# Attention of a decoder layer in float32: a query pair's high and low parts by one 128-row instruction each, placed by transfers

## The chip, the cores and the metric

One NeuronCore of a Trainium2 chip runs the whole kernel. The metric is the device time of one execution in microseconds (us).

## The reference, cut to what matters

A decoder layer on x of shape (4, 512, 512): self-attention, a cross-attention on 64 tokens, and a top-2 mixture of 8 experts, each behind a layer norm. Only the self-attention is touched:

```python
HQ, HKV, HD = (32, 8, 64)
q = (x @ Wq.T).reshape(B, L, HQ, HD)
k = (x @ Wk.T).reshape(B, L, HKV, HD)
v = (x @ Wv.T).reshape(B, L, HKV, HD)
q = _rope(q)
k = _rope(k)
...
attn = jnp.einsum('bkgqd,bkld->bkgql', qh, kh) * SCALE
attn = jnp.where(causal[None, None, None], attn, -jnp.inf)
p = jax.nn.softmax(attn, axis=-1)
out = jnp.einsum('bkgql,bkld->bkgqd', p, vh)
...
return out @ Wo.T
```

## The kernel before, in words

**Numbers in two parts.** TensorE multiplies in a shorter float format (fp32r), so each operand is split: a high part, which is a copy rounded to that format, and a low part, the value less its high part, rounded again. A product is the sum of the products of parts.

**Order of the work.** The attention stage runs over 8 groups (one key and value head and its 4 query heads), in each over 4 batches, in each over 4 query heads, 128 heads in all. Here `g` is the group, `b` the batch in it, `h` the head in it, `m = 4 g + b` the batch counted through, `n` the head counted through. Every engine has its own program, `pe_group`, `act_group`, `dve_group` and `pool_group`, which states the order of its steps head by head; they meet in semaphores only. The steps are staggered: while TensorE makes the scores of head n + 1, the probabilities of head n are transposed and the output of head n - 1 is made.

**A head's chain.** Scores on TensorE (`pe_scores`, line 207), in four row blocks of 512, 384, 256 and 256 columns into three banks. VectorE adds the causal mask and takes the row's extreme (`dve_masked`, line 421), four instructions. ScalarE takes the exponential (`act_exp`, line 312). VectorE inverts the sums (`dve_recip`, line 428), once per head. GpSimd scales (`pool_norm`, line 545). TensorE transposes ten blocks (`pe_ptrans`, line 217) in three units 0, 1 and 2, of which 0 and 2 share a bank. ScalarE takes the high part of each unit (`act_pt`), VectorE the low part (`dve_pt`, line 409, tile `pt_lo`). TensorE multiplies with v (`pe_pv`, line 234). The output product (`pe_wo`, line 246) follows per batch. In VectorE's order unit 2 of the head before stands behind the masked reductions of the next, and TensorE's unit 0 waits for it.

**The projections.** The next batch's products with the weights (`pe_proj`, line 184) are issued behind the scores of heads 0, 1 and 2: key and value rows (r = 0), the first pair of query heads (r = 1), the second pair (r = 2). As the weights' rows are laid out here `pe_proj` with index 2 is issued at head 0. Head 3 has no projection, but a short transpose of v (`pe_vt`). Rotation of a pair: VectorE multiplies by the cosine and swaps neighbouring rows (`dve_rope_in`, lines 439 and 440), GpSimd multiplies by the sine and adds (`pool_rope`, lines 536 and 538). The result `rope` holds two heads: 64 rows each.

**The query tile.** `q_st` holds for each of the four heads 128 rows: high part and low part, 64 rows each, so that one matmul with the key part takes both. In the first head of a pair the high part lies in rows 0 to 63, in the second in rows 64 to 127; the low part in the other half. `act_rope` (line 315) with r = 1 or 2 writes the high parts with two ScalarE copies of 64 rows (lines 324 and 325). `dve_q_lo` (line 442) writes the low parts with two VectorE subtractions of 64 rows (lines 446 and 447), of which each moves its result to the other half. It stands in VectorE's order behind the masked reductions, `dve_pt` of unit 2 and the low part of an output (`dve_o`, tile `o_lo`), and in front of `dve_rope_in`. The pair r = 1 of the next batch is made in head 2 and needed by the scores issued in head 3; the pair r = 2 of the present batch is made in head 0 and needed by the scores issued in head 1. `pe_scores` waits for `q_lo_done`.

**Weights.** SP loads a group's raw weights (`sp_w1`, `sp_w2`, lines 581 and 587) as soon as the raw tile is free, in a loop over groups; the high and low parts are made in group slots, the low parts of the query, key and value weights by GpSimd (`w1_lo`, line 456, in slots of batch 2), those of the output weights by VectorE in head 2 of batch 1 (`dve_w2`).

**The loop.** Group 0 and group 7 are written out. Groups 1 to 6 are a hardware loop of two passes over three groups each (lines 634, 667, 709, 738): the three probability buffers turn with the head, and 16 heads are one more than a multiple of three.

Of the kernel before, what the change touches and what calls it, by code (L numbers as in the profile page):

```python
# [15 lines left out]
F32 = mybir.dt.float32  # L16
F32R = mybir.dt.float32r
# [4 lines left out]
ALU = mybir.AluOpType  # L22
# [3 lines left out]
P = 128  # L26
# [72 lines left out]
def decoder_layer(nc, x, ctx, ctx_cols, mem_mask, wqkv, wo_rows, router_cols, router_b, gu_w, gu_b, down_w, down_b,  # L99
                  cos_t, sin_t, causal_t, ident_t, iota_t, out):  # L100
    stack = ExitStack()
    with stack:
# [24 lines left out]
        def sa(name, shape, dt=F32):  # L127
# [10 lines left out]
        probs = sa("probs", [P, 3, P_LEN])  # L138
        pt = [[sa(f"pt{b}_hi", [P, PT_LEN], F32R), sa(f"pt{b}_lo", [P, PT_LEN], F32R)] for b in range(2)]
        q_st = sa("q_st", [P, G, L], F32R)  # L140
        k_hi = sa("k_hi", [P, 2, L], F32R)
        k_lo = sa("k_lo", [P, 2, L], F32R)
        v_st = sa("v_st", [P, 2, QB, P], F32R)
# [14 lines left out]
            "const_in", "ident_in", "x_first", "x_in0", "x_in1", "x_in2", "x_in3", "zero_done", "half_done",  # L158
            "stat_done", "aggr_done", "eps_done", "rstd_done", "norm_done", "lnt_done", "ln_hi", "ln_lo",
            "w1_in", "w2_in", "w1_hi_done", "w1_lo_done", "w2_hi_done",  # L160
            "w2_lo_done", "proj_done", "vt_done", "rope_in", "rot_sin", "rope_sum", "rope_hi", "k_lo_done", "q_lo_done",
            "v_tr", "v_hi_done", "v_lo_done", "scores_done", "masked_done", "exp_done",
            "recip_done", "pnorm_done", "ptrans_done", "pt_hi_done", "pt_lo_done", "pv_done", "opart_done",
            "oadd_done", "o_hi_done", "o_lo_done", "wo_done", "wo_out_done")}
# [32 lines left out]
        def pe_scores(pe, n, m, h, kb):  # L197

            pe.wait_ge(s["k_lo_done"], 2 * m + 2)
            pe.wait_ge(s["q_lo_done"], 2 * m + 1 + (h >= 2))  # L200
            for k, blocks in enumerate(((3,), (2,), (1, 0))):
                wait(pe, s["masked_done"], 4 * n - (3, 2, 0)[k])
                for i in blocks:
                    cols = P * (i + 1) if i else 2 * P
                    at = 2 * P if i == 0 else 0
                    for a, kk in enumerate((k_hi, k_lo)):
                        last = nc.tensor.matmul(S_BANK[k][:, at:at + cols], q_st[:, h, i * P:(i + 1) * P], kk[:, kb, 0:cols],  # L207
                                                start=(a == 0), stop=(a == 1))
                last.then_inc(s["scores_done"], 1)
# [105 lines left out]
        def act_rope(act, m, r, mb):  # L315

            act.wait_ge(s["rope_sum"], 3 * m + r + 1)
            if r == 0:
                wait(act, s["scores_done"], 12 * m - 12)
                act_split(k_hi[0:HD, mb, :], rope[0:HD, mb, :], s["rope_hi"])  # L320
                act_split(k_hi[HD:P, mb, :], rope[0:HD, mb, :], s["rope_hi"])
            else:
                wait(act, s["scores_done"], 12 * m - 12 + 6 * r)
                act_split(q_st[0:HD, 2 * r - 2, :], rope[0:HD, (mb + r) % 2, :], s["rope_hi"])
                act_split(q_st[HD:P, 2 * r - 1, :], rope[HD:P, (mb + r) % 2, :], s["rope_hi"])

        def act_vt(act, m, r_sem_value):
            act.wait_ge(s["proj_done"], r_sem_value)
# [112 lines left out]

        def dve_q_lo(dve, m, r, mb):

            dve.wait_ge(s["rope_hi"], 6 * m + 2 * r + 2)
            a, c = 2 * r - 2, 2 * r - 1
            nc.vector.tensor_tensor(q_st[HD:P, a, :], rope[0:HD, (mb + r) % 2, :], q_st[0:HD, a, :].bitcast(F32), ALU.subtract)
            nc.vector.tensor_tensor(q_st[0:HD, c, :], rope[HD:P, (mb + r) % 2, :], q_st[HD:P, c, :].bitcast(F32), ALU.subtract).then_inc(s["q_lo_done"], 1)

        def dve_v(dve, m, vb):
            dve.wait_ge(s["v_hi_done"], m + 1)  # L450
# [95 lines left out]

        def pool_k_lo(pool, m, mb):

            pool.wait_ge(s["rope_hi"], 6 * m + 2)
            wait(pool, s["pnorm_done"], 16 * m - 8)  # L550
            for half_ in range(2):
                nc.gpsimd.tensor_tensor(k_lo[half_ * HD:(half_ + 1) * HD, mb, :], rope[0:HD, mb, :], k_hi[0:HD, mb, :].bitcast(F32),
                                        ALU.subtract).then_inc(s["k_lo_done"], 1)
            pool.wait_ge(s["k_lo_done"], 2 * m + 2)
# [26 lines left out]
        def sp_w1(sp, g):  # L581
# [2 lines left out]
                settled(sp)  # L584
            sp.dma_start(w1_raw[:, :, :], wqkv[bass.ds(g * P, P), :, :]).then_inc(s["w1_in"], 16)

        def sp_w2(sp, g):
            wait(sp, s["w2_lo_done"], 2 * g)
            if not isinstance(g, int):
                settled(sp)  # L590
            sp.dma_start(w2_raw[:, :, :], wo_rows[bass.ds(g * P, P), :, :]).then_inc(s["w2_in"], 16)

        with nc.Block() as block:

            @block.sync
            def _(sp):
                sp.dma_start(x_res[:, 0:1, :], xr[:, 0:1, :]).then_inc(s["x_first"], 16)
                sp.dma_start(x_res[:, 1:QB, :], xr[:, 1:QB, :]).then_inc(s["x_in0"], 16)
                sp_w1(sp, 0)
                for b in range(1, B):  # L600
                    sp.dma_start(x_res[:, b * QB:(b + 1) * QB, :], xr[:, b * QB:(b + 1) * QB, :]).then_inc(s[f"x_in{b}"], 16)
                    if b == 1:
                        sp.dma_start(cos[:, :], cos_t).then_inc(s["const_in"], 16)
                        sp.dma_start(sin[:, :], sin_t).then_inc(s["const_in"], 16)
                sp.dma_start(causal[:, :], causal_t).then_inc(s["const_in"], 16)
                sp_w2(sp, 0)
                with sp.Fori(1, GROUPS) as g:
                    sp_w1(sp, g)
                    sp_w2(sp, g)

            @block.tensor
            def _(pe):
                pe.wait_ge(s["ident_in"], 16)
                pe.wait_ge(s["zero_done"], 4)
                for t in range(TT):
                    pe_ln(pe, t)
                    if t == 6:
                        pe.wait_ge(s["w1_lo_done"], 3)
                        pe.wait_ge(s["ln_lo"], QB)
                        pe_proj(pe, 0, 2)  # L620
                    if t == 9:
                        pe.wait_ge(s["rope_in"], 1)
                        pe.wait_ge(s["vt_done"], 1)
                        pe_proj(pe, 0, 0)
                    if t == 12:
                        pe.wait_ge(s["rope_in"], 2)
                        pe_proj(pe, 0, 1)
                    if t == 14:
                        pe.wait_ge(s["rope_in"], 3)
                        pe_vt(pe, 0)  # L630
                pe.wait_ge(s["ln_lo"], TT)
                pe_scores(pe, 0, 0, 0, 0)
                pe_group(pe, 0, 0)
                with pe.Fori(0, (GROUPS - 2) // 3) as q:
                    for i in range(1, 4):
                        pe_group(pe, 3 * q + i, i % 3)
                pe_group(pe, GROUPS - 1, (GROUPS - 1) % 3)
                pe_ptrans(pe, HEADS * GROUPS - 1, (HEADS * GROUPS - 1) % 3, 2)
                pe_pv(pe, HEADS * GROUPS - 1, B * GROUPS - 1, 1, 1)
                pe_wo(pe, B * GROUPS - 2, 0, 3)  # L640
                for t in range(QB):
                    pe_wo(pe, B * GROUPS - 1, 1, t, (*S_BANK, PJ_BANK)[t])

            @block.scalar
            def _(act):
# [18 lines left out]
                act_rope(act, 0, 2, 0)  # L664
                act_exp(act, 0, 0)
                act_group(act, 0, 0)
                with act.Fori(0, (GROUPS - 2) // 3) as q:
                    for i in range(1, 4):
                        act_group(act, 3 * q + i, i % 3)
                act_group(act, GROUPS - 1, (GROUPS - 1) % 3)  # L670
                act_pt(act, HEADS * GROUPS - 1, 1, 2)
                act_opart(act, HEADS * GROUPS - 1)
# [3 lines left out]
            def _(dve):  # L676
# [29 lines left out]
                dve_masked(dve, 0, 0)  # L706
                dve_recip(dve, 0, 0)
                dve_group(dve, 0, 0)
                with dve.Fori(0, (GROUPS - 2) // 3) as q:
                    for i in range(1, 4):  # L710
                        dve_group(dve, 3 * q + i, i % 3)
                dve_group(dve, GROUPS - 1, (GROUPS - 1) % 3)
                dve_pt(dve, HEADS * GROUPS - 1, 1, 2)
                dve_oadd(dve, HEADS * GROUPS - 1, 1, HEADS * GROUPS // 2 - 1)
# [5 lines left out]
            @block.gpsimd  # L720
            def _(pool):
                nc.gpsimd.memset(half[:, :], -0.5).then_inc(s["half_done"], 1)
                pool.wait_ge(s["half_done"], 1)
                for t in range(TT):
                    wait(pool, s["lnt_done"], t - 1)
                    ln_norm(nc, pool, s, "", t, x_res[:, t, :], ln_out[:, t % 2, 0:D], var_eps, half, rstd)
                    if t == 10:
                        pool.wait_ge(s["const_in"], 48)
                        pool_rope(pool, 0, 0, 0)
                    if t == 12:  # L730
                        pool.wait_ge(s["norm_done"], 13)
                        pool_k_lo(pool, 0, 0)
                    if t == 14:
                        pool_rope(pool, 0, 1, 0)
                pool_rope(pool, 0, 2, 0)
                pool_norm(pool, 0, 0)
                pool_group(pool, 0, 0)
                with pool.Fori(0, (GROUPS - 2) // 3) as q:
                    for i in range(1, 4):
                        pool_group(pool, 3 * q + i, i % 3)  # L740
                pool_group(pool, GROUPS - 1, (GROUPS - 1) % 3)

        attn.close()
# [894 lines left out]
```

## Time and profile before

| | |
|---|---|
| median of 3 runs | 1640.2 us (1631.22, 1640.2, 1640.63) |
| the profiled execution | 1635.06 us |
| its span, first to last instruction | 1633.3 us |
| TensorE matmul (PE) busy | 1483.1 us, 91% |
| TensorE weight load (PEld) busy | 1306.6 us, 80% |
| VectorE (DVE) busy | 1372.1 us, 84% |
| ScalarE (ACT) busy | 1057.7 us, 65% |
| GpSimd (POOL) busy | 849.6 us, 52% |

The attention stage takes the first two thirds of the span. Matmuls overlap and their ends are modelled, so a busy TensorE is not one at its peak. "SPq" is SP's queue, which issues the transfers. In groups by line the last columns are the busy time, the mean of one instruction, and the time that the engine stood idle just before these instructions with what ended most of it. In the timeline "[1.51 <-DVE pt_lo L409]" is idle time before the instruction and what ended it. The granted clock (PEclk) is TensorE's, as a share of its full speed of 2.4 GHz.

### The profile page before, as it was taken

Reading aid. Unit: us, or ns where it says so; the run is one execution under the profiler, and the core shown is the slowest. Engines: PE = TensorE matmul, PEld = TensorE weight load, DVE = VectorE, ACT = ScalarE, POOL = GpSimd, SP = SyncE. Lnnn points to the kernel's source line nnn. Section 1 sums busy time; section 2 is a strip of 40 time slices with the busy share of each in tenths; the row PEclk is TensorE's granted clock in tenths of the full one; section 3 lists DMA queues with packets and bytes.
Section 4 is the critical chain, followed back from the end, with each engine's and each line's share of the span. In section 5 each row is a group of like instructions: output and inputs, shape, how many; then the busy total and the mean of one; then the engine's idle time right before and its main releaser. Section 6 shows DMA issues by size and latency. Waiting matters only on the chain. (4 is left out here: it accounts for less than half of the span.)

```text
span 1633.3 us, 31312 instructions
## 1 busy us (share of the span) xinstructions
PE 1483.1 (91%) x8951; PEld 1306.6 (80%) x8951; DVE 1372.1 (84%) x3565; ACT 1057.7 (65%) x2464; POOL 849.6 (52%) x1033
## 2 busy tenths in 40 slices
PE   5789999999999899999999999688599999999994
PEld 4678888888888788878878877577489999999993
DVE  7789888898898788988988988577579988998892
ACT  3677777777777677777777777332166666666661
POOL 6667657657657557657657655267612233222321
PEclk9899999999999999999999999967599999999997
DMA  4000000000000000000000000112468778887765
GB/s 175 1 14 20 1 14 21 1 14 21 1 14 20 3 14 21 2 14 21 1 14 1 1 1 1 41 65 92 164 184 243 226 217 220 240 228 219 198 172 135
DMA packets 62032, 124.97 MB, mean 77 GB/s; under 512 B 20942, under 2 KB 21070, under 8 KB 61792
## 3 DMA queue, kind: packets, MB, share of 16 engines
q1 hardware_dynamic: 51408, 102.24, 19.6%
q0 software_dynamic: 10304, 20.59, 6.6%
q8 instruction: 77, 1.26, 0.3%
q14 instruction: 99, 0.81, 0.2%
q10 hardware_dynamic: 144, 0.07, 0.0%
HBM read 106.08 MB, written 24.71 MB: 80 GB/s over the span
## 5 line engine op out<-in xcount | busy, mean ns | idle before, releaser
L312 ACT ACTIVATE probs<-probs,neg_max 128x512 f32<-128x512 f32 (+3 forms) x512 | 281.7, 552 | 46.5 <-DVE neg_max L421 44.2
L545 POOL TENSOR_SCALAR probs<-probs,row_inv 128x512 f32<-128x512 f32 (+3 forms) x512 | 264.3, 535 | 44.4 <-DVE row_inv L428 44.4
L536 POOL TENSOR_TENSOR rot<-rot,sin 128x512 f32<-128x512 f32 (+1 forms) x96 | 123.6, 1288 | 303.4 <-DVE rot L440 299.1
L217 PE MATMUL bank<-ident,probs 128*128 128x128 f32 x1280 | 184.5, 275 | 59.6 <-DVE pt_lo L409 50.1
L409 DVE TENSOR_TENSOR pt_lo<-bank,pt_hi 128x512 fp32r<-128x512 f32 (+1 forms) x384 | 216.3, 591 | 25.8 <-ACT pt_hi L305 25.7
L305 ACT ACTIVATE pt_hi<-bank 128x512 fp32r<-128x512 f32 (+1 forms) x384 | 186.3, 518 | 71.6 <-PE bank L217 63.6
L421 DVE CUSTOM_DVE_ANT_0 probs<-bank,causal 128x512 f32<-128x512 f32 (+3 forms) x512 | 219.7, 482 | 10.1 <-issue 3.6
L1221 POOL DMA_INDIRECT acc<-ctx_raw,idx x46 | 74.5, 1619 | 294.9 <-ACT ctx_raw L1374 280.8
L217 PEld LDWEIGHTS bank<-ident,probs 128*128 128x128 f32 x1280 | 149.9, 140 | 94.9 <-DVE pt_lo L409 54.9
L1302 PE MATMUL bank<-xt_hi,gu_hi 128*128 128x256 f32 x736 | 208.4, 283 | 2.0 <-DVE xt_lo L409 1.5
L1302 PE MATMUL bank<-xt_lo,gu_hi 128*128 128x256 f32 x736 | 206.7, 281 | 0.0
L1302 PE MATMUL bank<-xt_hi,gu_lo 128*128 128x256 f32 x736 | 206.5, 281 | 0.0
L207 PE MATMUL bank<-k_hi,q_st 128*128 128x256 f32 (+2 forms) x512 | 172.3, 347 | 3.2 <-DVE xn_lo L409 3.2
L234 PE MATMUL bank<-pt_hi,v_st 128*128 128x256 f32 (+2 forms) x512 | 171.4, 346 | 1.6 <-DVE pt_lo L409 1.6
L207 PE MATMUL bank<-k_lo,q_st 128*128 128x256 f32 (+2 forms) x512 | 156.9, 328 | 0.0
L234 PE MATMUL bank<-pt_lo,v_st 128*128 128x256 f32 (+2 forms) x512 | 155.8, 326 | 0.0
L184 PE MATMUL bank<-xn_hi,w_hi 128*128 128x512 f32 x384 | 153.2, 399 | 0.4 <-DVE rot L440 0.4
L184 PE MATMUL bank<-xn_lo,w_hi 128*128 128x512 f32 x384 | 151.9, 396 | 0.0
L184 PE MATMUL bank<-xn_hi,w_lo 128*128 128x512 f32 x384 | 151.5, 395 | 0.0
L1302 PEld LDWEIGHTS bank<-xt_hi,gu_hi 128*128 128x128 f32 x736 | 139.2, 189 | 6.2 <-issue 2.8
L1302 PEld LDWEIGHTS bank<-xt_lo,gu_hi 128*128 128x128 f32 x736 | 139.5, 189 | 2.8
L1302 PEld LDWEIGHTS bank<-xt_hi,gu_lo 128*128 128x128 f32 x736 | 139.1, 189 | 0.0
(196 smaller groups left out, 3912.8 us busy)
## 6 DMA issues: line engine op xcount, KB each, us to landing
gu_raw<-in_gate_up SPq DMA_DIRECT2D x92, 512.0 KB, 4.2
dn_raw<-in_down SPq DMA_DIRECT2D x92, 256.0 KB, 3.8
w_raw<-in_wqkv SPq DMA_DIRECT2D x8, 768.0 KB, 4.1
w_raw<-in_wo_rows SPq DMA_DIRECT2D x8, 512.0 KB, 3.5
h_rows<-ln_h SPq DMA_DIRECT2D x16, 256.0 KB, 2.0
acc<-x_res SPq DMA_DIRECT2D x4, 1024.0 KB, 4.7
x_res<-in_x SPq DMA_DIRECT2D x3, 1024.0 KB, 11.4
ctx_raw<-in_ctx SPq DMA_DIRECT2D x2, 512.0 KB, 6.7
```

Source lines behind the costliest of these rows:

```text
L184: last = nc.tensor.matmul(PJ_BANK[:, :], w1[sp][:, c, r * P:(r + 1) * P], xn[mp][:, c, b * L:(b + 1) * L], start=first, stop=(c == DC - 1 ...
L207: last = nc.tensor.matmul(S_BANK[k][:, at:at + cols], q_st[:, h, i * P:(i + 1) * P], kk[:, kb, 0:cols], start=(a == 0), stop=(a == 1))
L217: last = nc.tensor.transpose(T_BANK[u % 2][:, k * P:(k + 1) * P], probs[:, hb, P_AT[i] + j * P:P_AT[i] + (j + 1) * P], ident[:, :])
L234: last = nc.tensor.matmul(dst, v_st[:, vb, j, :], rhs, start=(j == 0 and a == 0), stop=(j == QB - 1 and a == 1))
L305: nc.scalar.activation(dst, src, ACT.Copy).then_inc(sem_, 1)
L312: nc.scalar.activation(row, row, ACT.Exp, bias=neg_max[:, hb, i:i + 1], scale=-1.0, accum_out=row_sum[:, hb, i:i + 1]).then_inc(s["exp_don ...
L409: nc.vector.tensor_tensor(dst, src, hi.bitcast(F32), ALU.subtract).then_inc(sem_, 1)
L421: nc.vector.tensor_tensor_reduce(out=probs[:, hb, P_AT[i]:P_AT[i] + (i + 1) * P], in0=S_BANK[k][:, at:at + (i + 1) * P], in1=causal[:, (QB ...
L536: nc.gpsimd.tensor_tensor(rot[0:rows, :], rot[0:rows, :], sin[0:rows, :], ALU.mult).then_inc(s["rot_sin"], 1)
L545: nc.gpsimd.tensor_scalar(row, row, row_inv[:, hb, i:i + 1], 0.0, ALU.mult, ALU.add).then_inc(s["pnorm_done"], 1)
L1221: nc.gpsimd.indirect_dma_start(out=acc, out_offset=bass.IndirectOffsetOnAxis(ap=idx[:, 2 * tau + h:2 * tau + h + 1], axis=0), in_=y[:, 2 * ...
L1302: last = nc.tensor.matmul(GU_BANK[u % 3][:, side * TILE:(side + 1) * TILE], gu[sp_][:, ib, c, side, :], xts[mp][:, k, c, :], start=first, ...
```

## The change

Each part of a query pair is now made by one instruction over all 128 rows, into two new tiles, `q_two` high and low, in the order in which `rope` holds the pair. ScalarE copies the high part, VectorE subtracts the low part, and then SP issues four transfers of 64 rows from `q_two` to the places in `q_st` (`sp_q`). The scores wait for these transfers, `q_in1` or `q_in2`, in place of `q_lo_done`. The wait for the scores that last read `q_st` moves from ScalarE to SP; ScalarE waits for the transfers that last read `q_two`. The loops over groups are written out on all engines, and SP's program is an order by batches, in which the weights' loads stand between the query transfers. Since q's high parts have a semaphore of their own, `pool_k_lo` waits for another count. The same four lines stand in the programs of ScalarE, VectorE and GpSimd as shown for TensorE.

```diff
--- before.py
+++ after.py
@@ -138,6 +138,7 @@
         probs = sa("probs", [P, 3, P_LEN])
         pt = [[sa(f"pt{b}_hi", [P, PT_LEN], F32R), sa(f"pt{b}_lo", [P, PT_LEN], F32R)] for b in range(2)]
         q_st = sa("q_st", [P, G, L], F32R)
+        q_two = [sa("q_two_hi", [P, L], F32R), sa("q_two_lo", [P, L], F32R)]
         k_hi = sa("k_hi", [P, 2, L], F32R)
         k_lo = sa("k_lo", [P, 2, L], F32R)
         v_st = sa("v_st", [P, 2, QB, P], F32R)
@@ -158,7 +159,7 @@
             "const_in", "ident_in", "x_first", "x_in0", "x_in1", "x_in2", "x_in3", "zero_done", "half_done",
             "stat_done", "aggr_done", "eps_done", "rstd_done", "norm_done", "lnt_done", "ln_hi", "ln_lo",
             "w1_in", "w2_in", "w1_hi_done", "w1_lo_done", "w2_hi_done",
-            "w2_lo_done", "proj_done", "vt_done", "rope_in", "rot_sin", "rope_sum", "rope_hi", "k_lo_done", "q_lo_done",
+            "w2_lo_done", "proj_done", "vt_done", "rope_in", "rot_sin", "rope_sum", "rope_hi", "k_lo_done", "q_hi_done", "q_lo_done", "q_in1", "q_in2",
             "v_tr", "v_hi_done", "v_lo_done", "scores_done", "masked_done", "exp_done",
             "recip_done", "pnorm_done", "ptrans_done", "pt_hi_done", "pt_lo_done", "pv_done", "opart_done",
             "oadd_done", "o_hi_done", "o_lo_done", "wo_done", "wo_out_done")}
@@ -197,7 +198,7 @@
         def pe_scores(pe, n, m, h, kb):
 
             pe.wait_ge(s["k_lo_done"], 2 * m + 2)
-            pe.wait_ge(s["q_lo_done"], 2 * m + 1 + (h >= 2))
+            pe.wait_ge(s["q_in2" if h >= 2 else "q_in1"], 64 * m + 64)
             for k, blocks in enumerate(((3,), (2,), (1, 0))):
                 wait(pe, s["masked_done"], 4 * n - (3, 2, 0)[k])
                 for i in blocks:
@@ -320,9 +321,11 @@
                 act_split(k_hi[0:HD, mb, :], rope[0:HD, mb, :], s["rope_hi"])
                 act_split(k_hi[HD:P, mb, :], rope[0:HD, mb, :], s["rope_hi"])
             else:
-                wait(act, s["scores_done"], 12 * m - 12 + 6 * r)
-                act_split(q_st[0:HD, 2 * r - 2, :], rope[0:HD, (mb + r) % 2, :], s["rope_hi"])
-                act_split(q_st[HD:P, 2 * r - 1, :], rope[HD:P, (mb + r) % 2, :], s["rope_hi"])
+                if r == 2:
+                    act.wait_ge(s["q_in1"], 64 * m + 64)
+                else:
+                    wait(act, s["q_in2"], 64 * m)
+                act_split(q_two[0][:, :], rope[:, (mb + r) % 2, :], s["q_hi_done"])
 
         def act_vt(act, m, r_sem_value):
             act.wait_ge(s["proj_done"], r_sem_value)
@@ -441,10 +444,8 @@
 
         def dve_q_lo(dve, m, r, mb):
 
-            dve.wait_ge(s["rope_hi"], 6 * m + 2 * r + 2)
-            a, c = 2 * r - 2, 2 * r - 1
-            nc.vector.tensor_tensor(q_st[HD:P, a, :], rope[0:HD, (mb + r) % 2, :], q_st[0:HD, a, :].bitcast(F32), ALU.subtract)
-            nc.vector.tensor_tensor(q_st[0:HD, c, :], rope[HD:P, (mb + r) % 2, :], q_st[HD:P, c, :].bitcast(F32), ALU.subtract).then_inc(s["q_lo_done"], 1)
+            dve.wait_ge(s["q_hi_done"], 2 * m + r)
+            dve_lo(q_two[1][:, :], rope[:, (mb + r) % 2, :], q_two[0][:, :], s["q_lo_done"])
 
         def dve_v(dve, m, vb):
             dve.wait_ge(s["v_hi_done"], m + 1)
@@ -546,7 +547,7 @@
 
         def pool_k_lo(pool, m, mb):
 
-            pool.wait_ge(s["rope_hi"], 6 * m + 2)
+            pool.wait_ge(s["rope_hi"], 2 * m + 2)
             wait(pool, s["pnorm_done"], 16 * m - 8)
             for half_ in range(2):
                 nc.gpsimd.tensor_tensor(k_lo[half_ * HD:(half_ + 1) * HD, mb, :], rope[0:HD, mb, :], k_hi[0:HD, mb, :].bitcast(F32),
@@ -584,6 +585,15 @@
                 settled(sp)
             sp.dma_start(w1_raw[:, :, :], wqkv[bass.ds(g * P, P), :, :]).then_inc(s["w1_in"], 16)
 
+        def sp_q(sp, m, r):
+
+            sp.wait_ge(s["q_lo_done"], 2 * m + r)
+            wait(sp, s["scores_done"], 12 * m - 12 + 6 * r)
+            a, c = 2 * r - 2, 2 * r - 1
+            for dst, of in ((q_st[0:HD, a, :], q_two[0][0:HD, :]), (q_st[HD:P, a, :], q_two[1][0:HD, :]),
+                            (q_st[0:HD, c, :], q_two[0][HD:P, :]), (q_st[HD:P, c, :], q_two[1][HD:P, :])):
+                sp.dma_start(dst.bitcast(F32), of.bitcast(F32)).then_inc(s[f"q_in{r}"], 16)
+
         def sp_w2(sp, g):
             wait(sp, s["w2_lo_done"], 2 * g)
             if not isinstance(g, int):
@@ -604,9 +614,15 @@
                         sp.dma_start(sin[:, :], sin_t).then_inc(s["const_in"], 16)
                 sp.dma_start(causal[:, :], causal_t).then_inc(s["const_in"], 16)
                 sp_w2(sp, 0)
-                with sp.Fori(1, GROUPS) as g:
-                    sp_w1(sp, g)
-                    sp_w2(sp, g)
+                sp_q(sp, 0, 1)
+                sp_q(sp, 0, 2)
+                for m in range(1, B * GROUPS):
+                    if m % B == 1 and m // B + 1 < GROUPS:
+                        sp_w1(sp, m // B + 1)
+                    if m % B == 3 and m // B + 1 < GROUPS:
+                        sp_w2(sp, m // B + 1)
+                    sp_q(sp, m, 1)
+                    sp_q(sp, m, 2)
 
             @block.tensor
             def _(pe):
@@ -631,9 +647,8 @@
                 pe.wait_ge(s["ln_lo"], TT)
                 pe_scores(pe, 0, 0, 0, 0)
                 pe_group(pe, 0, 0)
-                with pe.Fori(0, (GROUPS - 2) // 3) as q:
-                    for i in range(1, 4):
-                        pe_group(pe, 3 * q + i, i % 3)
+                for g in range(1, GROUPS - 1):
+                    pe_group(pe, g, g % 3)
                 pe_group(pe, GROUPS - 1, (GROUPS - 1) % 3)
                 pe_ptrans(pe, HEADS * GROUPS - 1, (HEADS * GROUPS - 1) % 3, 2)
                 pe_pv(pe, HEADS * GROUPS - 1, B * GROUPS - 1, 1, 1)
...
```

## Rows read from the trace of the kernel before

**Rows 1.** Busy time by stretch: us, PE, PEld, DVE, ACT, POOL (instructions), PEclk, DMA, GB/s.
```profile
275.00:375.00 100.00, 95.94 (x551) 83.18 (x551) 88.85 (x241) 76.56 (x193) 63.23 (x82) 1.00 0.02 7
```

**Rows 2.** Groups by line, 75 to 1100 us: count, busy us, mean ns, idle before.
```profile
L217 PE MATMUL bank<-ident,probs 128*128 128x128 f32 x1260 | 181.5, 275 | 55.7 <-DVE pt_lo L409 46.2 <-POOL probs L545 8.8 <-issue 0.5
...
L305 ACT ACTIVATE q_st<-rope 64x512 fp32r<-64x512 f32 x122 | 76.4, 626 | 2.2
...
L409 DVE TENSOR_TENSOR o_lo<-o_f,o_hi 128x512 fp32r<-128x512 f32 x64 | 46.9, 733 | 0.7 <-ACT o_hi L305 0.7
```

**Rows 3.** Timeline, batch 2's heads 0 and 1: start us, us, engine, line, operation.
```profile
356.35 0.48 PE L207 MATMUL bank<-k_hi,q_st 128*128 128x512 f32 x1
...
357.20 0.69 DVE L421 CUSTOM_DVE_ANT_0 probs<-bank,causal 128x512 f32<-128x512 f32 x1
...
359.90 0.68 DVE L446 TENSOR_TENSOR q_st<-rope,q_st 64x512 fp32r<-64x512 f32 x1
...
364.12 0.48 PE L207 MATMUL bank<-k_hi,q_st 128*128 128x512 f32 x1
```

**Rows 4.** Timeline, a group's batch 0, heads 2 and 3.
```profile
313.97 0.69 DVE L446 TENSOR_TENSOR q_st<-rope,q_st 64x512 fp32r<-64x512 f32 x1
...
318.11 0.48 PE L207 MATMUL bank<-k_hi,q_st 128*128 128x512 f32 x1
...
319.08 0.67 DVE L421 CUSTOM_DVE_ANT_0 probs<-bank,causal 128x512 f32<-128x512 f32 x1
```

**Rows 5.** Timeline, the same group's batch 1, heads 2 and 3, with SP's queue.
```profile
344.19 0.69 DVE L446 TENSOR_TENSOR q_st<-rope,q_st 64x512 fp32r<-64x512 f32 x1
...
345.61 1.29 DVE L409 TENSOR_TENSOR w_lo<-w_raw,w_hi 128x512 fp32r<-128x512 f32 x2
...
347.13 0.33 SPq L591 DMA_DIRECT2D w_raw<-in_wo_rows  x1
...
349.15 0.49 PE L207 MATMUL bank<-k_hi,q_st 128*128 128x512 f32 x1
...
350.50 0.67 DVE L421 CUSTOM_DVE_ANT_0 probs<-bank,causal 128x512 f32<-128x512 f32 x1
```

**Rows 6.** Timeline, the same group's batch 2, heads 2 and 3.
```profile
375.00 1.72 POOL L456 TENSOR_TENSOR w_lo<-w_raw,w_hi 128x512 fp32r<-128x512 f32 x1
...
375.61 1.66 DVE L446 TENSOR_TENSOR q_st<-rope,q_st 64x512 fp32r<-64x512 f32 x1
...
380.33 0.49 PE L207 MATMUL bank<-k_hi,q_st 128*128 128x512 f32 x1
```

**Rows 7.** DMA issues, and stretches: a 128-partition store, the 64-partition ctx loads.
```profile
h_rows<-ln_h SPq DMA_DIRECT2D x16, 256.0 KB, 2.0
...
1076.71:1076.96 0.25, 0.25 (x5) 0.25 (x4) 0.25 (x3) 0.25 (x2) 0.21 (x1) 1.00 1.00 385
...
1057.20:1057.60 0.40, 0.00 (x0) 0.00 (x0) 0.00 (x0) 0.00 (x0) 0.40 (x2) 0.50 1.11 215
```

**Rows 8.** Timeline, the first and last pair: q's low part, then scores or reduction.
```profile
44.90 0.68 DVE L446 TENSOR_TENSOR q_st<-rope,q_st 64x512 fp32r<-64x512 f32 x1
...
48.03 0.80 PE L207 MATMUL bank<-k_hi,q_st 128*128 128x512 f32 x1 [3.22 <-DVE xn_lo L409]
...
1010.87 0.68 DVE L446 TENSOR_TENSOR q_st<-rope,q_st 64x512 fp32r<-64x512 f32 x1
...
1014.81 0.67 DVE L421 CUSTOM_DVE_ANT_0 probs<-bank,causal 128x512 f32<-128x512 f32 x1
```

**Rows 9.** Reciprocals of groups 3, 4 and 5, and a stretch after the restart.
```profile
414.92 0.18 DVE L428 RECIPROCAL row_inv<-row_sum 128x4 f32<-128x4 f32 x1 [0.99 <-ACT probs L312]
...
537.94 0.18 DVE L428 RECIPROCAL row_inv<-row_sum 128x4 f32<-128x4 f32 x1 [0.99 <-ACT probs L312]
...
666.52 0.18 DVE L428 RECIPROCAL row_inv<-row_sum 128x4 f32<-128x4 f32 x1 [0.99 <-ACT probs L312]
...
553.00:556.00 3.00, 3.00 (x12) 2.67 (x11) 3.00 (x11) 2.53 (x6) 2.92 (x6) 0.56 0.00 0
```

More of the change, by code:

```diff
@@ L666, in _ @@
                 act_group(act, 0, 0)
-                with act.Fori(0, (GROUPS - 2) // 3) as q:
-                    for i in range(1, 4):
-                        act_group(act, 3 * q + i, i % 3)
+                for g in range(1, GROUPS - 1):
+                    act_group(act, g, g % 3)
                 act_group(act, GROUPS - 1, (GROUPS - 1) % 3)
@@ L708, in _ @@
                 dve_group(dve, 0, 0)
-                with dve.Fori(0, (GROUPS - 2) // 3) as q:
-                    for i in range(1, 4):
-                        dve_group(dve, 3 * q + i, i % 3)
+                for g in range(1, GROUPS - 1):
+                    dve_group(dve, g, g % 3)
                 dve_group(dve, GROUPS - 1, (GROUPS - 1) % 3)
@@ L737, in _ @@
                 pool_group(pool, 0, 0)
-                with pool.Fori(0, (GROUPS - 2) // 3) as q:
-                    for i in range(1, 4):
-                        pool_group(pool, 3 * q + i, i % 3)
+                for g in range(1, GROUPS - 1):
+                    pool_group(pool, g, g % 3)
                 pool_group(pool, GROUPS - 1, (GROUPS - 1) % 3)
```

## The prediction

> **What bounds the kernel now.** I read the busy time by stretches first: in 100 us from the middle of the attention stage TensorE is busy for 95.94 us, VectorE for 88.85, ScalarE for 76.56, at a granted clock of 1.00 [rows 1]. So TensorE bounds this stage and VectorE stands close behind it. Then the groups of instructions by line: the only work that TensorE waits for is the transpose of the probabilities, 55.7 us of idle time in front of it, 46.2 of them until VectorE's pt_lo [rows 2]. The timeline says where. A batch is four heads of one group of weights. Heads 0 to 2 issue a projection of the next batch behind their scores; head 3 has none, and there TensorE stands until VectorE has done the head's four masked reductions and pt_lo. That is a wait on VectorE's order of work; it shrinks only as far as the masked reductions start sooner.
>
> One measure is used all through: S, the start of a head's scores on TensorE, and M, the start of its masked reductions on VectorE. Where VectorE is free in time M is S + 0.85 (357.20 less 356.35) [rows 3].
>
> **The change part by part.** *VectorE, q's low part.* Two 64-row subtractions of about 0.69 us [rows 3] become one of 128 rows; the same subtraction over 128 rows in the output stage, also from SBUF to SBUF, takes 0.73 in the mean [rows 2]. So some 0.69 us go per pair of heads, 64 times, 44 us of VectorE's time. Most of it was never waited for. Where it counts is head 3, since head 2 carries one of the pairs and VectorE reaches head 3's masked reductions late: M is S + 0.97 in batch 0 of a group (319.08 less 318.11) [rows 4] and S + 1.35 in batch 1 (350.50 less 349.15) [rows 5]. With 0.69 us less ahead of it, M falls to S + 0.85: 0.12 us gained in batches 0 and 3, 0.50 in batch 1, and the same 0.5 in batch 2, which is as crowded. After that the scores themselves are the bound.
>
> *ScalarE, q's high part.* Two copies of 0.626 us [rows 2] become one of 128 rows. Its cost lies between 0.63 (rows cost nothing, as on VectorE) and 1.25 (rows cost in full); I take 0.63. Either way it ends well ahead of VectorE's masked reductions and the o_lo that stand in front of q's low part, so it is off the path: 0.
>
> *The four transfers.* This is the new link. Before, the scores could start when the second subtraction ended; now SP must see the semaphore, issue four transfers of 64 rows x 2 KB (128 KB each), and all four must land. The new subtraction stands where L446 stood, so its end is L446's end. The time that it leaves until S, if S is to stay:
> - head 0 to head 1, every batch: 364.12 - 360.58 = 3.54 us [rows 3];
> - head 2 to head 3, batches 0 and 3: 318.11 - 314.66 = 3.45 [rows 4];
> - batch 1: 349.15 - 344.88 = 4.27, two VectorE steps of w_lo stand between [rows 5];
> - batch 2: 380.33 - 377.27 = 3.06, because the subtraction takes 1.66 there [rows 6].
>
> No row of this trace is a transfer from SBUF to SBUF, so the latency is put together. SP's wake: w_lo ends at 346.90 and SP issues at 347.13, 0.23 [rows 5]. A 256 KB store from SBUF lands 2.0 us after its issue and moves at 385 GB/s while it runs [rows 7], so 0.68 us is data and 1.32 is fixed. Four transfers are 524 KB. At 385 GB/s that is 1.36 us; at the 215 GB/s at which the two 64-partition loads of ctx ran, one half of the partitions behind the other on one queue [rows 7], it is 2.44. Ends: 0.23 + 1.32 + 1.36 = 2.9 us and 0.23 + 1.32 + 2.44 = 4.0 us; three later issues at the 0.33 of one [rows 5] fit beside the data in both. I take 4.0: rows 7's loads are the only ones with 64 partitions on the SBUF side, as each of these has on both sides. Then, per pair:
> - head 1: 4.0 - 3.54 = 0.46 late, on an engine that was never idle there, so 0.46 lost; 30 times (31 later batches less the last): +13.8;
> - head 3, batches 0 and 3 and the last group's batch 2 (no weights follow there): 4.0 - 3.45 - 0.12 = +0.43, 16 times: +6.9;
> - head 3, batch 1: q lands at 348.88, 0.27 ahead of the old S, and M gains 0.50: -0.77, 8 times: -6.2. TensorE is ready for it, since the output product that waited for w_lo in front starts earlier too;
> - head 3, batch 2: 4.0 - 3.06 - 0.52 = +0.42, 7 times: +2.9.
>
> Sum +17.4 us. At the start of the stage the first pair's subtraction ends at 45.58, so S goes from 48.03 to 49.6 [rows 8]: +1.5. At the end the last one ends at 1011.55; q lands at 1015.55 and M goes from 1014.81 to 1016.4 [rows 8]: +1.6.
>
> The subtraction of batch 2 takes 1.66 us exactly while GpSimd runs w_lo on two SBUF inputs, itself 1.72 us [rows 6]. By the Trainium skill (SBUF — State Buffer, "SBUF: two separate sides") a VectorE operation with two SBUF inputs and a GpSimd operation exclude each other on a shared port for the whole instruction; the trace agrees. The new subtraction still has two SBUF inputs and the same neighbour, so I leave the 1.66; without it the sum would be 7 us lower.
>
> *The loop written out.* The heads' period does not differ between looped and written-out groups. Only the second pass of the loop costs: from its first reciprocal to the next group's group 3 takes 123.02 us (414.92 to 537.94), group 4 takes 128.58 (537.94 to 666.52) [rows 9]. All engines jump back there. That goes: -5.6, if the straight code is fetched ahead, as in the first and last groups, which are written out before too.
>
> *SP's queue and the added waits.* ScalarE's new wait is for transfers of the pair two heads back: 0. The wait for the scores that last read q_st moves from ScalarE to SP, behind the wait for the subtraction, and is by then long met; POOL's queue keeps its order, only a semaphore's count changes: 0. The weight loads now go between the q transfers, behind a pair's four and two heads ahead of the next: 0, or the sub-microsecond of one issue. On TensorE everything behind the scores (projection, output product, transposes) waits with them; that is why lateness counts in full.
>
> Sum: +17.4 + 1.5 + 1.6 - 5.6 = +14.9 us on the profiled execution's 1635.1 (span 1633.3): **1650**. The median of the three runs, 1640.2, lies 5 us above that execution, so on another day this may read 1655. A measurement of this kernel tells about 1%, 16 us, from no change.
>
> **Rivals.**
> 1. *The transfers are hidden: faster.* If the four run at 385 GB/s (latency 2.9), nothing is late except at the ends (+0.5 and +0.5). Head 3 then gains 0.12 x 16 + 1.05 x 8 + 0.6 x 7 = 14.5 (batch 1's S moves up to where TensorE is free, 0.55; batch 2's by 0.1): -14.5 + 1.0 - 5.6 = -19, 1616 us. For it: two of the four read the lower rows and write the upper or the reverse, so reads and writes could overlap. Against: the halves of ctx came no faster for following each other [rows 7]. It decides at a latency of 3.75, where the sum is zero; each 0.1 us of latency is worth 61 x 0.1 = 6 us.
> The Trainium skill (DMA: Bandwidth & Descriptors, "Rules for kernel authors") says of two transfers to disjoint partition halves that they serialize, and to use one of 128 partitions. By that rule the four add up; the ctx row agrees.
> 2. *The transfers are later still: clearly slower.* Nothing in the trace shows reading 64 partitions and writing 64 at once, or four back-to-back issues. If a start of each costs SP or the queue another 0.2 us, the latency is 4.6 and the sum 15 + 61 x 0.6 = +52: 1687. For it: four transfers behind one semaphore, the last one counts. Against: three issues of 0.33 fit beside the data. It makes the kernel slower from a latency of 3.75 on, and by over 1% from about 4.02 on.
> 3. *The clock falls.* After the loop's restart the granted clock was 0.56 for 3 us [rows 9], so 1.3 us lost per fall. If lateness and the wait of head 3 together did that in every batch: 31 x 1.3 = 40 on top, 1690. Against: head 3's present waits leave the clock at 1.00 [rows 1].
>
> **How the numbers follow.** My forecast (latency 3.7 to 4.3) 0.45, rival 1 (below 3.7) 0.25, rival 2 0.25, rival 3 0.05. Over 1% faster needs a latency under 3.5: half of rival 1, 0.12. Over 1% slower: rivals 2 and 3 and a third of the forecast, which begins at a latency of 4.02 in my sum, 0.45. The rest, 0.43, within 1%. Range: from rival 1's near end, 1622, to rival 2, 1690; the forecast alone is 1632 to 1668.
>
> **What would show it.** Right: TensorE idle in front of the scores (L207) until a transfer, about 0.5 us at heads 1 and 3, none at head 3 of batch 1; the four transfers landing some 3.7 us after the first issue; 64 subtractions of about 0.69, seven of 1.66; group 4 as long as groups 3 and 5. Wrong: no idle time in front of L207 (then the time is near 1616), or a microsecond and more of it; a group 4 that is still longer; a granted clock below 1.00 in the middle.

## The result, and the profile after

The changed kernel takes 1662.3 us (median of 4 runs, 1660.1 to 1664.3) against 1638.0 for the kernel before (1631.2 to 1640.6): ratio 1.017, interval 1.014 to 1.019. It is slower by 1.7%, where +0.9% (14.9 us) had been forecast. The profiled executions differ by the same: spans of 1660.6 and 1633.3 us, 27.3 apart, at a granted clock of 0.955 in both. So 27.3 us is what has to be found.

Measured from the start of one head's scores to the next (S, as in the prediction), all of it lies in the attention stage. The first scores start 1.7 us later, groups 0 to 7 take 25.8 us more, and from the last scores to the end of the kernel both take 611 us.

The kernel after, busy time by stretch, same columns and stretch as [rows 1]:

```profile
275.00:375.00 100.00, 93.58 (x536) 80.67 (x535) 82.02 (x222) 69.15 (x179) 59.01 (x76) 1.00 0.20 50
```

VectorE fell from 88.85 us to 82.02, ScalarE from 76.56 to 69.15: the instructions that were to go are gone (over the whole span VectorE runs 3501 in place of 3565, ScalarE 2400 in place of 2464). Yet TensorE, which bounds the stage, does less in the same time. The clock stays at 1.00. Where TensorE stands idle, the groups of instructions by line say (kernel after, 75 to 1100 us; columns as in [rows 2]):

```profile
L218 PE MATMUL bank<-ident,probs 128*128 128x128 f32 x1261 | 180.6, 274 | 40.4 <-DVE pt_lo L412 33.7 <-POOL probs L546 6.8
L208 PE MATMUL bank<-k_hi,q_st 128*128 128x512 f32 x496 | 164.5, 343 | 37.7 <-issue 37.7
L412 DVE TENSOR_TENSOR q_two_lo<-rope,q_two_hi 128x512 fp32r<-128x512 f32 x61 | 41.7, 684 | 0.0
L306 ACT ACTIVATE q_two_hi<-rope 128x512 fp32r<-128x512 f32 x61 | 38.1, 624 | 0.0
```

Two things are to be seen. The wait in front of the transposes (L218 here, L217 before) shrank from 55.7 us [rows 2] to 40.4: VectorE's relief at head 3. And a group that never waited, the scores (L208, L207 before), has 37.7 us of idle time in front of it. "issue" there means that the profile shows no releaser; the timeline names it. Both new instructions of 128 rows take what one of 64 rows took (684 and 624 ns).

The kernel after, timeline: batch 1's head 3 with its transfers, batch 2's heads 0 and 1, then heads 2 and 3, in the group of [rows 4 to 6]. Columns: start us, us, engine, line, operation, and in brackets the idle time before it:

```profile
353.85 0.68 DVE L412 TENSOR_TENSOR q_two_lo<-rope,q_two_hi 128x512 fp32r<-128x512 f32 x1
...
354.56 0.46 SPq L595 DMA_DIRECT2D q_st<-q_two_hi  x1
...
355.07 0.60 SPq L595 DMA_DIRECT2D q_st<-q_two_lo  x1
...
355.71 0.60 SPq L595 DMA_DIRECT2D q_st<-q_two_hi  x1
...
356.35 0.60 SPq L595 DMA_DIRECT2D q_st<-q_two_lo  x1
...
358.76 0.47 PE L208 MATMUL bank<-k_hi,q_st 128*128 128x512 f32 x1 [0.29 <-issue]
...
365.53 0.48 PE L208 MATMUL bank<-k_hi,q_st 128*128 128x512 f32 x1
...
368.95 0.69 DVE L412 TENSOR_TENSOR q_two_lo<-rope,q_two_hi 128x512 fp32r<-128x512 f32 x1
...
373.85 0.47 PE L208 MATMUL bank<-k_hi,q_st 128*128 128x512 f32 x1 [0.30 <-issue]
...
384.32 1.29 POOL L457 TENSOR_TENSOR w_lo<-w_raw,w_hi 128x512 fp32r<-128x512 f32 x1
384.47 1.69 DVE L412 TENSOR_TENSOR o_lo<-o_f,o_hi 128x512 fp32r<-128x512 f32 x1
386.08 0.68 DVE L412 TENSOR_TENSOR q_two_lo<-rope,q_two_hi 128x512 fp32r<-128x512 f32 x1
...
391.04 0.47 PE L208 MATMUL bank<-k_hi,q_st 128*128 128x512 f32 x1 [1.34 <-issue]
```

From the subtraction's end to the scores it is 358.76 - 354.53 = 4.23 us, then 373.85 - 369.64 = 4.21; the median is 4.25. (The idle times in brackets count from the modelled end of the matmul before, which overlaps with its successor, so they show less than S loses.) The steps of the first one: SP issues 0.03 after the end; its four issues take 0.46 and three times 0.60, and stand 0.51, 0.64 and 0.64 apart; the fourth starts 1.82 after the subtraction's end. One transfer lands 2.3 us after its own issue (the page's list of DMA issues):

```profile
q_st<-q_two_hi SPq DMA_DIRECT2D x128, 128.0 KB, 2.3
q_st<-q_two_lo SPq DMA_DIRECT2D x128, 128.0 KB, 2.3
```

0.03 + 1.79 + 2.3 + 0.1 for TensorE's start = 4.2. So it is the fourth issue that comes late. While the train runs, the data moves at the rate of the narrow ctx loads, 215 GB/s here (kernel after, stretch, columns as in [rows 1]); but 128 KB each 0.64 us is 205 GB/s, so this rate alone doesn't say whether the issues or the data set the pace:

```profile
356.00:356.20 0.20, 0.20 (x3) 0.20 (x2) 0.20 (x1) 0.20 (x1) 0.00 (x0) 1.00 1.01 215
```

Intervals of S, medians over groups 1 to 6, in us:

| interval | before | after | change |
|---|---|---|---|
| head 0 to 1, every batch | 7.77 | 8.37 | +0.59 |
| head 1 to 2, every batch | 7.82 | 7.80 | -0.01 |
| head 2 to 0, batches 0 and 3 | 14.62 | 15.11 | +0.48 |
| head 2 to 0, batch 1 | 15.83 | 15.11 | -0.73 |
| head 2 to 0, batch 2 | 15.61 | 16.12 | +0.52 |

That is 4 x 0.59 - 4 x 0.01 + 2 x 0.48 - 0.73 + 0.52 = 3.1 us more per group. Beside these medians some trains of four are stretched: the second issue takes between 0.65 and 1.57 us in place of 0.60, and the scores are late by as much more. One of them (kernel after, timeline):

```profile
306.42 0.46 SPq L595 DMA_DIRECT2D q_st<-q_two_hi  x1
306.92 1.29 SPq L595 DMA_DIRECT2D q_st<-q_two_lo  x1
308.26 0.60 SPq L595 DMA_DIRECT2D q_st<-q_two_hi  x1
...
311.37 0.47 PE L208 MATMUL bank<-k_hi,q_st 128*128 128x512 f32 x1 [1.19 <-issue]
```

There are ten such trains; their second issues are together 5.3 us longer than ten of 0.60. Five other trains are late by 0.2 to 0.7 us, some 1.8 us in all, by a fourth issue that starts later or a last landing that takes up to 3.0 us; why, no run here shows. The loop's restart is gone: the reciprocals that start groups 3, 4 and 5 stand 126.75 and 127.19 us apart, where they stood 123.02 and 128.58 apart [rows 9]:

```profile
426.29 0.18 DVE L431 RECIPROCAL row_inv<-row_sum 128x4 f32<-128x4 f32 x1 [0.98 <-ACT probs L313]
...
553.04 0.18 DVE L431 RECIPROCAL row_inv<-row_sum 128x4 f32<-128x4 f32 x1 [0.99 <-ACT probs L313]
...
680.23 0.18 DVE L431 RECIPROCAL row_inv<-row_sum 128x4 f32<-128x4 f32 x1 [0.99 <-ACT probs L313]
```

### The profile page after: what moved, and what is told of

Read it like the earlier page. It is cut to its first block and busy times, and to the rows that moved or that the text cites. A ratio compares the mean times of both kernels' runs of the same rounds, so it can differ in the third digit from the quotient of the medians.

```text
span 1660.6 us, 28906 instructions
## 1 busy us (share of the span) xinstructions
PE 1489.5 (90%) x8951; PEld 1308.6 (79%) x8951; DVE 1325.6 (80%) x3501; ACT 1014.0 (61%) x2400; POOL 843.9 (51%) x1033
## 5 line engine op out<-in xcount | busy, mean ns | idle before, releaser
L218 PE MATMUL bank<-ident,probs 128*128 128x128 f32 x1280 | 183.3, 274 | 44.3 <-DVE pt_lo L412 37.5
L218 PEld LDWEIGHTS bank<-ident,probs 128*128 128x128 f32 x1280 | 151.9, 141 | 73.7 <-POOL probs L546 26.2
L208 PE MATMUL bank<-k_hi,q_st 128*128 128x256 f32 (+2 forms) x512 | 171.1, 345 | 42.3 <-issue 37.7
L208 PE MATMUL bank<-k_lo,q_st 128*128 128x256 f32 (+2 forms) x512 | 156.5, 327 | 0.0
L306 ACT ACTIVATE v_and_o<-bank 64x512 f32<-64x512 f32 x160 | 95.1, 594 | 84.6 <-PE bank L235 74.6
L208 PEld LDWEIGHTS bank<-k_hi,q_st 128*128 128x128 f32 x512 | 97.4, 190 | 61.0 <-issue 55.4
```

The source lines that it names most:

```text
L218: last = nc.tensor.transpose(T_BANK[u % 2][:, k * P:(k + 1) * P], probs[:, hb, P_AT[i] + j * P:P_AT[i] + (j + 1) * P], ident[:, :])
L306: nc.scalar.activation(dst, src, ACT.Copy).then_inc(sem_, 1)
```

## The experiments

The theory after the result: the scores are late because four transfers, issued one behind the other and only when the subtraction has ended, land 0.5 us or so past the time at which TensorE wants them. Rivals: it is the transfers' load, not their lateness; it is their half width of 64 partitions; it is the written-out loop.

**1. The loop alone.** The kernel before, loop written out on all engines:

```
-                with pe.Fori(0, (GROUPS - 2) // 3) as q:
-                    for i in range(1, 4):
-                        pe_group(pe, 3 * q + i, i % 3)
+                for g in range(1, GROUPS - 1):
+                    pe_group(pe, g, g % 3)
```

> The kernel before with its loops over groups written out on all engines, and nothing else. Theory (the lateness of the four transfers costs the time, the straight code gains): group 4 falls from 128.6 to 123.0 us, so 5.6 us less, 0.3% faster. Rival (straight code has a price of its own, such as waits for code in every group): no gain or a loss, groups of 124 us and more, as the groups of the changed kernel vary from 126.3 to 128.4.

Measured: 1632.9 us against 1636.8, ratio 0.998 (0.996 to 0.999): a gain of 4 us, between 1.5 and 6.7. The 5.6 us of the restart lie inside. The profiled execution is the longest of the 13 (1643.6 us): in it groups 3 and 4 take the same 124.7 us, so the restart is gone, but the 123.0 expected of group 4 is not to be seen there. Six of its heads lose 1.6 us each at a lower granted clock (last section), one of them in group 3 and one in group 4; the groups without such a head, 5 and 6, take 123.1. So the written-out loop doesn't slow the kernel; the other part costs all of the loss and what the loop gives.

**2. The pairs and transfers alone.** The kernel after, with the loops of the four compute engines put back (the edit above, reversed).

> The changed kernel with the loops over groups put back on TensorE, VectorE, ScalarE and GpSimd; SP's program stays written out. Theory: 5.6 us above the changed kernel, some 2.0% slower than before; the waits in front of the scores stay as they are. Rival: at or below the changed kernel, because the straight code cost something.

Measured: 1680.3 us, ratio 1.028 (1.025 to 1.032). The sign is right, the size isn't: this is 18 us above the kernel after, not 5.6. The restart is worth some 3 us of it (group 4 takes 131.3, the others 128.4 to 129.3). Ten trains are stretched here too, but by 9.1 us in all in place of 5.3, one issue to 1.96 us. And the median from subtraction to scores is 4.37 us in place of 4.25, though the transfers are no slower: from the subtraction's end to the last landing it is 4.15 in both kernels, but TensorE starts 0.19 us after that landing in place of 0.09. So in looped code each late pair is later still on TensorE's side; why, no run here settles.

**3. The high parts sent ahead.** SP sends the two high transfers as soon as ScalarE has made them; two are left behind the subtraction:

```
+            sp.wait_ge(s["q_hi_done"], 2 * m + r)
+            wait(sp, s["scores_done"], 12 * m - 12 + 6 * r)
+            ...    two transfers from q_two[0]
             sp.wait_ge(s["q_lo_done"], 2 * m + r)
-            wait(sp, s["scores_done"], 12 * m - 12 + 6 * r)
-            ...    four transfers
+            ...    two transfers from q_two[1]
```

> The changed kernel, but SP issues the two transfers of the high parts as soon as ScalarE has made them, and only the two of the low parts behind the subtraction. Theory: the latency behind the subtraction falls from 4.2 to about 2.9 us (half of the data, 1.25 us less), under the 3.5 us there are; no idle time in front of the scores, group of about 120.8 us, 1.1 to 1.3% faster than before. Rival (the transfers cost by being there, not by being late): about the changed kernel's time, 1.5% slower than before.

Measured: 1618.9 us, ratio 0.989 (0.987 to 0.991), as the theory said. Same four transfers, same bytes, same VectorE: only two issues fewer in the chain. Groups by line (75 to 1100 us) of this kernel:

```profile
L208 PE MATMUL bank<-k_hi,q_st 128*128 128x512 f32 x492 | 163.5, 343 | 1.5 <-issue 1.5
```

37.7 us of idle time became 1.5. Head 0 to 1 is back at 7.77, a group takes 121.1 us.

**4. The subtraction earlier.** VectorE's q_lo of both pairs stands ahead of o_lo (`dve_o`), transfers as in the kernel after:

```
-                if d_begun and dh % 2 == 1 and ...:
-                    dve_o(dve, ...)
                 if h == 0 and begun and front:
                     dve_q_lo(dve, m, 2, b % 2)
                 if h == 2 and next_batch:
                     dve_q_lo(dve, m + 1, 1, (b + 1) % 2)
+                if d_begun and dh % 2 == 1 and ...:
+                    dve_o(dve, ...)
```

> The changed kernel, but VectorE makes q's low part ahead of the output's low part o_lo in place of behind it, so 0.69 us sooner. Theory: the 4.2 us now begin 0.69 us sooner, so the scores at head 1 are no longer late (7.8 us after those of head 0, from 8.35) and those at head 3 hardly; about 25 us less than the changed kernel, at or slightly under the time of before. Rival (a fixed cost of the transfers, or a wait of TensorE for o_lo that takes its place): less than 8 us gained.

Measured: 1634.0 us, ratio 0.998 (0.996 to 1.000), so 28 us under the kernel after. Head 0 to 1 is 7.77 again. The subtraction ends 3.51 us behind the previous scores in place of 4.11, so 0.60 sooner. The start of the chain works as well as its length: it is lateness against one point in time. What remains late are batch 2's head 3 (8.77 us behind head 2, 8.40 in the kernel before) and the stretched trains.

**5. Full width, four transfers.** Each of 128 partitions and half the columns, the same bytes:

```
-            ((q_st[0:HD, a, :], q_two[0][0:HD, :]), ...)
+            for at, k in ((a, 0), (a, 1), (c, 0), (c, 1)):
+                cols = ...    the k-th half of the columns
+                sp.dma_start(q_st[:, at, cols], q_two[k][:, cols])
```

> The changed kernel, but each of the four transfers takes 128 partitions of 1 KB in place of 64 of 2 KB: the same bytes, four issues, one queue. It puts the parts in the wrong halves, so the scores are other numbers. Theory (64 partitions move at half the rate): data at 380 to 390 GB/s in place of 205, all four in 1.4 us; the latency falls from 4.2 to between 3.1 and 3.8 us according to how fast SP can issue, scores of head 1 between 7.8 and 8.0 us after head 0, 0 to 1% faster than before. Rival (a transfer inside SBUF moves at some 205 GB/s in any shape, or four issues are the bound): latency 4.0 or more, 1.2% or more slower than before.

Measured: 1649.0 us, ratio 1.007 (1.005 to 1.010); from subtraction to scores 4.02 us. The theory was wrong; of the rival its second half was right (four issues are the bound, 4.0 us or more), though not its 1.2%. Timeline, and stretches of the same train (columns as in [rows 1]):

```profile
321.61 0.68 DVE L412 TENSOR_TENSOR q_two_lo<-rope,q_two_hi 128x512 fp32r<-128x512 f32 x1
...
322.32 0.47 SPq L596 DMA_DIRECT2D q_st<-q_two_hi  x1
322.83 0.60 SPq L596 DMA_DIRECT2D q_st<-q_two_lo  x1
323.48 0.60 SPq L596 DMA_DIRECT2D q_st<-q_two_hi  x1
324.12 0.60 SPq L596 DMA_DIRECT2D q_st<-q_two_lo  x1
...
326.28 0.47 PE L208 MATMUL bank<-k_hi,q_st 128*128 128x512 f32 x1
```

```profile
323.60:323.80 0.20, 0.20 (x2) 0.17 (x1) 0.20 (x2) 0.20 (x1) 0.00 (x0) 1.00 0.99 343
323.80:324.00 0.20, 0.20 (x3) 0.20 (x3) 0.20 (x3) 0.20 (x1) 0.07 (x1) 1.00 0.31 92
...
324.20:324.40 0.20, 0.20 (x4) 0.20 (x3) 0.20 (x2) 0.00 (x0) 0.20 (x1) 1.00 0.99 343
```

The data now runs at 343 GB/s with gaps between, and the issues still stand 0.64 apart. So the issues set the pace; the width is worth 0.23 us, in the last transfer alone.

**6. Full width, two transfers** of 128 partitions and all columns (`for at, k in ((a, 0), (c, 1))`).

> The changed kernel with two transfers of 128 partitions of 2 KB in place of the four (only the first head's high-part tile and the second head's low-part tile are placed, whole; the scores are other numbers). Same bytes, half the issues, full width. Theory: latency about 2.9 us, nothing late, head 1's scores 7.77 us after head 0's, about 1620 us. Rival (205 GB/s in any shape): 4.0 us, about 1655 us.

Measured: 1619.2 us in one execution. Two stretches, in the first transfer and in the second:

```profile
326.80:327.00 0.20, 0.20 (x4) 0.20 (x3) 0.17 (x2) 0.00 (x0) 0.01 (x1) 1.00 1.00 379
327.40:327.60 0.20, 0.20 (x5) 0.20 (x3) 0.00 (x0) 0.20 (x1) 0.20 (x1) 1.00 0.95 369
```

Half the issues, the same bytes at 369 to 379 GB/s, head 0 to 1 at 7.77: nothing is late but batch 2's head 3 (8.20, where run 7 without a wait has 7.81). The Trainium skill (DMA: Bandwidth & Descriptors, "Rules for kernel authors") advises one transfer over 128 partitions in place of two over halves; the trace agrees with the advice, and run 5 shows that here most of the gain is the number of issues: of the 43 us between the kernel after and this run, the width with four issues had given 13.

**7. No wait for the transfers.** The scores read a tile that never changes; the transfers run as in the kernel after (one wait for all of them stands at the end of the stage):

```
-            pe.wait_ge(s["q_in2" if h >= 2 else "q_in1"], 64 * m + 64)
...
-   ... q_st[:, h, i * P:(i + 1) * P] ...
+   ... xn[0][:, h, i * P:(i + 1) * P] ...
```

> The changed kernel with all its transfers, but the scores read a tile of layer norm outputs that stays as it is, in place of the placed queries, and do not wait for the transfers (the scores are other numbers). It is the price of everything but the lateness. Theory: no idle time before the scores, group of 120.8 to 121.2 us, 1.1 to 1.3% faster than before, as with the high parts sent early. Rival (the transfers or the straight code slow other work): at or above 1630 us.

Measured: 1617.5 us, ratio 0.987 (0.983 to 0.992). Two reciprocals that start neighbouring groups in this kernel's timeline, 120.96 us apart:

```profile
419.92 0.15 DVE L430 RECIPROCAL row_inv<-row_sum 128x4 f32<-128x4 f32 x1
...
540.88 0.15 DVE L430 RECIPROCAL row_inv<-row_sum 128x4 f32<-128x4 f32 x1
```

Every transfer is made, some trains are stretched here too (an issue of 1.44 us), and none of it shows in the groups: they take what rival 1 gives for hidden transfers (123.0 less some 1.9). So no price of the load is to be seen; the wait is the price.

**8. Runs 3 and 4 together.**

> High parts sent early and the low part made ahead of o_lo, both together. Theory (once nothing is late, more room is worth nothing): the same as with the high parts sent early alone, 1.1% faster than before, within 0.3%; only head 3 of batch 2, 8.06 to 8.09 us in that run, falls to 7.8, 2 us in all. Rival (the rest of head 3's wait still hangs on the transfers): another 0.5% or more.

Measured: 1613.9 us, ratio 0.985 (0.982 to 0.989), the fastest of all: some 22 us under the kernel before. A group takes 121.0 us, as with no wait at all, though in one train the two low issues take 2.62 us in place of 1.10: there is now room for it. It is 0.4% under run 3, where at most 0.3% was expected, but the intervals overlap. Groups 1 to 6 are only 0.2 us shorter than in run 3, the first and the last group 2.5 and 2.2.

## Why the prediction was right and wrong

**Right: what bounds, and why the kernel gets slower.** TensorE bounds the stage and lateness of the transfers counts in full; runs 3, 4 and 7 each take the lateness away by other means, and each gets back the loss. Head 3 got its relief from VectorE: batch 1 gained 0.73 us per group (0.77 forecast). Batches 0 and 3 lost 0.48 each (0.43). The start lost 1.7 (1.5). The restart of group 4 is gone (5.6; run 1 bears it out). ScalarE's copy of 0.62 us and VectorE's of 0.68 are the lower bounds taken. The two waits on VectorE's and ScalarE's side cost nothing to be seen.

**Wrong: the latency term, "three later issues at the 0.33 of one fit beside the data".** It gave 0.23 + 1.32 + 2.44 = 4.0 us. The 0.33 came from a single load; three later issues in a row take 0.60 and stand 0.51 to 0.64 apart, so they aren't beside the data but are the chain, 1.79 us long. The wake was less (0.03, not 0.23), one transfer's landing 2.3, and the whole 4.2 to 4.25. That the forecast's 4.0 came so near is luck: it had the width as the cause, which run 5 puts at 0.23 us. And by the prediction's own 6 us for each 0.1 us, these 0.25 us would have added 15; some 5 came, because the subtraction also ends sooner against the scores than the forecast had it. Rival 2 had named this mechanism (a start of each costs more) at a dearer price, 4.6 us.

Head 0 to 1 lost 0.59 us, not 0.46: the subtraction now ends 4.11 us behind the previous scores (369.64 - 365.53), where 360.58 - 356.35 = 4.23 had been carried over [rows 3], and 4.11 + 4.25 = 8.36. With batches 2 (0.52 for 0.42) and 0 and 3 that is 3.1 us per group in place of 2.35, some 5 of the 12.4 us by which the sum was short.

**Missing: the late trains,** some 7 us: 5.3 by the ten stretched ones, 1.8 by the five others. They stood at nothing; no term was there for a train that is now and then longer, on a chain without room. Each of the ten has one packet of an instruction queue (q8, 16 KB) that starts between 0.2 us before and 0.6 us after the train's first issue, and of the other 54 trains none has one while its issues run. In run 2, where two packets start 1.0 and 1.8 us after the first issue, it is the third and the fourth issue that is stretched. The DMA view of the stretch of the one shown above, 305 to 312 us: packets, MB, share of the engines:

```profile
q1 hardware_dynamic: 374, 0.86, 50.1%
q8 instruction: 1, 0.02, 1.2%
```

So the stretched issue goes with the packet. That the fetch causes it is not shown: no run took the fetches away, and in run 7 one of twelve trains with such a packet isn't stretched. With the some 5 us above, these 7 make up the 12.4.

**Wrong in place, right in price: batch 2's collision.** The subtraction of 1.66 us [rows 6] was to stay; it is 0.68 now. But o_lo in front of it takes 1.69 beside GpSimd's w_lo, and the delay reaches the scores all the same. In run 4, where the subtraction stands first, it is the subtraction again that takes 1.7, in seven batches. That is as the Trainium skill's rule cited in the prediction (SBUF — State Buffer, "SBUF: two separate sides") has it: the exclusion holds for whichever VectorE step with two SBUF inputs meets GpSimd's.

**The rivals.** The transfers weren't hidden (rival 1); run 3 and run 6 show what it would have given, 1619 us against its 1616. The clock stayed at 1.00 (rival 3).

## What to carry to other kernels

Price a chain of DMA issues by their spacing in a row (0.51 to 0.64 us each here), not by one isolated issue, and set the latency from producer to reader against the room between them in the timeline, with some to spare for a train that is late. Send each part as soon as it is made, in as few and as wide transfers as the layout allows, so that only the last part stands in the chain. An instruction halved on an engine that isn't the bound is worth only what its readers waited for; here it was paid for on the engine that is.

## What the runs showed of the hardware

Executions of the kernel before take from 1628.8 to 1647.9 us, and the longer ones have the lower mean granted clock (0.956 at 1631.4 us, 0.945 at 1641.7). Where such time can go is shown by run 1's profiled execution, 1643.6 us at 0.944. Its head 3 waits 1.7 us in front of the transposes in batches 1 and 2 of a group, and behind six of these 15 waits TensorE's granted clock falls from 1.00 to its lower level of 1.2 GHz (a mean of 0.72 over the 6 us shown below) and rises again while TensorE stays busy. In the profiled execution of the kernel before twelve of these waits are 1.5 us, three are 1.7, and the clock falls behind none of them; that the same falls make its longer executions long is argued, not shown. Timeline and stretches of run 1's kernel (columns as in [rows 1]):

```profile
357.56 1.94 PE L217 MATMUL bank<-ident,probs 128*128 128x128 f32 x8 [1.73 <-POOL probs L545]
```

```profile
355.00:361.00 6.00, 4.27 (x22) 3.84 (x22) 4.12 (x14) 3.76 (x11) 4.84 (x9) 0.72 0.00 0
361.00:367.00 6.00, 6.00 (x33) 5.12 (x33) 4.83 (x14) 4.64 (x12) 0.00 (x0) 1.00 0.00 0
```

Such a head takes 8.95 us in place of 7.36. Why the same wait costs the clock six times and not the other nine stays open.
